# State-space layer: B times the step by TensorE for four states of three channel groups, and the norm one chunk later

## The chip, the cores and the metric

The kernel runs on one core of one Trainium2 chip. The metric is the time of the whole program on the device, in microseconds (us), as the median of several runs.

## What is computed

The program is a tower of nine layers over 8 images of 257 tokens with 256 channels. The change lies in one of them, a bidirectional state-space layer: the same recurrence runs over the tokens forward and backward, with weights of its own for each direction. Cut to what matters:

```python
xz = einsum('bld,ed->ble', x, Win);  u, z = split(xz, 2)      # 512 channels each
uc = silu(conv4(u));  x_dbl = uc @ Wx.T                       # rank 16, B 32, C 32
dt = softplus(x_dbl[..., :16] @ Wdt.T + bdt)
def step(h, ins):                                             # h: 512 channels x 32 states
    dt_t, B_t, C_t, u_t = ins
    h = exp(dt_t[..., None] * A) * h + (dt_t * u_t)[..., None] * B_t[:, None, :]
    return h, einsum('bdn,bn->bd', h, C_t)
y = (scan(step) + uc * Dp) * silu(z);  out = y @ Wout.T       # then a layer norm and Wfuse
```

## The kernel before

The state-space layer is `section_mamba`. It has 16 **units** `u`: 8 images forward, then 8 backward. In a unit the 512 channels are 4 groups `j` of 128 (one channel to a partition), and the 32 states are taken two at a time, so that a unit has 64 **pairs** `p`, 16 for each group. Four pairs are a **chunk** `n`; a unit has 16 chunks, numbered 0 to 15, and the inner counter `m` is 0 to 3. The work of a pair goes through all engines:

- ScalarE, `decay`: two exponentials give the decay `da` of the pair, one chunk ahead of VectorE.
- TensorE, `spread_b`: two bf16 matmuls put the two rows of B on all partitions, into one of the four PSUM buffers `pb`. It waits until the scan of pair p-4 has freed the buffer, and stands two pairs ahead of VectorE in the program.
- VectorE, `product`: multiplies that buffer by `dtu` (the step times u). It stands one pair ahead of the scan, so that VectorE's order is product p+1, scan p.
- VectorE, `tensor_tensor_scan`: runs the recurrence along 256 tokens for both states, and frees the buffer (`b_free`).
- GpSimd: multiplies the result by C, two pairs at a time (`hc`).
- TensorE, `total`: adds the products of each state into `py`, two chunks behind.

Each engine has its own instruction list, executed in order, and the order is written out by hand in its `body`: at fixed places (n, m) the list of unit u also holds the preparation of unit u+1 (projections `project`, `b_c_rank`, `time_step`, convolution, softplus) and the rest of unit u-1 (`outward`, the norm's `variance`, `fuse`, and on ScalarE `take_out`, `square`, `root`, `affine`). Three places matter below:

- ScalarE opens chunk 7 with `take_out(u-1)`, which waits for TensorE's `outward` of chunk 6 (m = 3).
- ScalarE's `decay` calls in chunk 15 belong to chunk 0 of unit u+1, and the first waits for the step of the next unit (`dt_set`), which GpSimd makes in `soften` behind its own chunk 13.
- Units 1 to 6 and 9 to 14 stand in two loops of three rounds of two units.

The parts of ScalarE's list that the places stand in, as before:

```python
if n == 7 and before is not None:
    take_out(u - 1)
...
for m in range(4):
    ...
    if n + 1 < NCH:
        decay(u, v, d, n + 1, m, free)
    elif after is not None:
        decay(u + 1, 1 - v, after, 0, m, free)
```

Of the kernel before, what the change touches and what calls it, by code (L numbers as in the profile page):

```python
# [23 lines left out]
P = 128  # L24
B = 8
# [1195 lines left out]
def section_mamba(nc, k, con, dirs, bfuse, normed=0):  # L1221
# [5 lines left out]
    UN = 2 * B  # L1227
    L = T - 1
    open_section(nc, k, "mamba")
    with ExitStack() as ctx:  # L1230
# [22 lines left out]
        y_l = sb("yl", [P, 2, DJ])  # L1253
        e1, e2 = sb("e1", [P, DJ, T]), sb("e2", [P, DJ, T])
# [3 lines left out]
        names = ("w_first w_in w_ready eye_set rates in_back out_back x_in proj_done proj_free lead uc_done xd_done xd_out part_set part_cut stacked last_bc last_out rate_l decay_l sum_l y_last z_last dt_done "  # L1258
# [7 lines left out]
        def image(u, d):  # L1266
            return u - B * d

# [29 lines left out]
        with nc.Block() as block:  # L1298
            @block.sync
            def _(sp):  # L1300
# [8 lines left out]
                sp.wait_ge(s["xd_done"], B)  # L1309
                sp.wait_ge(s["dt_done"], DJ * B)  # L1310
# [144 lines left out]
            def _(pe):  # L1455
# [37 lines left out]
                def spread_b(u, v, p):  # L1493

                    pe.wait_ge(s["b_free"], Turn(u, SUB, 4)(p - 3))
                    for o in range(2):
                        st = 2 * (p % (NS_ // 2)) + o
                        ins = nc.tensor.matmul(pb[:, p % 4, o, :], one_state(st), bst2[:, v, 0:L], start=True, stop=True)  # L1498
                    ins.then_inc(s["b_done"], 1)

                def total(u, v, d, n, m):
# [38 lines left out]
                def body(u, v, d, before, after):  # L1540
# [4 lines left out]
                    for n in range(NCH):  # L1545
                        for m in range(4):
# [6 lines left out]
                            elif before is not None:  # L1553
                                total(u - 1, 1 - v, before, NCH - 2 + n, m)
                            if n < QN:
                                spread_c(u, v, NQ_ * n + 2 * m)
                                spread_c(u, v, NQ_ * n + 2 * m + 1)
                            if after is not None:
# [19 lines left out]
                                if (n, m) == (14, 2):  # L1578
# [3 lines left out]
                            if before is not None:  # L1582
# [11 lines left out]
                                if (n, m) == (12, 2):  # L1594
                                    fuse(u - 1, 1)
                                if (n, m) == (13, 0):
# [10 lines left out]
                b_c_rank(0, 0)  # L1607
                for j in range(DJ):
# [19 lines left out]
            def _(act):  # L1628
# [4 lines left out]
                act.sem_inc(s["c_free"], 2)  # L1633

# [16 lines left out]
                def take_rank(u):  # L1651
# [3 lines left out]
                    nc.scalar.copy(part[:, 0, :], rank[0:2 * NS_, :]).then_inc(s["part_set"], 1)  # L1655

# [69 lines left out]
                def body(u, v, d, before, after):  # L1726
                    for n in range(NCH):
# [6 lines left out]
                        if n == 11 and before is not None:  # L1734
                            root(u - 1)
                        if n == 12 and before is not None:
                            affine(u - 1, before)
                        for m in range(4):
# [5 lines left out]
                            if n < QN:  # L1744
                                for o in range(2):
                                    st = NQ_ * n + 2 * m + o
                                    act.wait_ge(s["c_done"], Turn(u, NS_)(st + 1))
                                    nc.scalar.copy(cb[:, st, :], pm[:, st % 2, 0:L]).then_inc(s["c_free"], 1)  # L1748
                        if n == 1 and before is not None:
                            decay_last(u - 1)  # L1750
                        if after is not None:
# [7 lines left out]
                            if n == 9:  # L1759
                                take_rank(u + 1)  # L1760
                            if n == 10:
# [20 lines left out]
                take_rank(0)  # L1782
                act.wait_ge(s["w_in"], 16 * 12)
# [20 lines left out]
            def _(dve):  # L1804
# [47 lines left out]
                def product(u, v, p):  # L1852

                    j = p // (4 * QN)
# [6 lines left out]
                def body(u, v, d, before, after):  # L1861
                    for n in range(NCH):
                        q = n % QN
                        j = n // QN
                        for m in range(4):
# [8 lines left out]
                            dve.wait_ge(s["b_set"], Turn(u, SUB)(p + 1))  # L1874
# [4 lines left out]
                            if before is not None:  # L1879
# [4 lines left out]
                                if (n, m) == (11, 2):  # L1884
                                    scale(u - 1)
                                if (n, m) == (13, 2):
# [959 lines left out]
```

## Time and profile before

| | |
|---|---|
| median of 3 runs | 4415.77 us (4385.23 to 4431.04) |
| the profiled execution | 4409.2 us, its span 4407.5 us |
| the state-space layer in it | about 1547 to 3349 us, 1802 us |
| busy in that stretch | VectorE 1793.5, GpSimd 1627.7, TensorE 1580.0, ScalarE 1361.2 us |

The page sums over nine layers; only the stretch of the state-space layer is touched, and it is read by itself. Records of TensorE overlap each other (a matmul's end is modelled), so its pace is read from one start to the next, and so is VectorE's.

### The profile page before, as it was taken

The numbers are of one execution on the slowest core, as the hardware profiler recorded it, in microseconds if no ns is written. First come the engines' busy times: TensorE is split into PE (matmuls) and PEld (weight loads), VectorE is DVE, ScalarE is ACT, GpSimd is POOL, SyncE is SP. The second block draws the span as 40 slices with busy tenths as digits, with TensorE's granted clock in tenths as the row PEclk, the third lists the DMA queues.
The fourth block names the chain that finished last, engine by engine and source line by source line (L and its number), as shares of the span: only waits on it lengthen the run. The fifth ranks groups of instructions, "written<-read, shape, count | busy, mean of one in ns | idle before, by whom it ended". The sixth has DMA issues, their size and how long they took to land. (4 is left out here: it accounts for less than half of the span.)

```text
span 4407.5 us, 60885 instructions
## 1 busy us (share of the span) xinstructions
PE 3597.4 (82%) x19446; PEld 2461.4 (56%) x19446; DVE 2653.6 (60%) x3903; ACT 2062.6 (47%) x4702; POOL 1824.5 (41%) x1794
## 2 busy tenths in 40 slices
PE   2848848988798688888888889888887788888857
PEld 1625527555665456666666666666655655555534
DVE  6322233444322399999999999999996333333331
ACT  1211111222311377777777777777773233343322
POOL 0030020000100289999899999999983000000011
PEclk9669967999999899999999999999999999999965
DMA  3137730000247300000000000000000000000045
GB/s 88 49 135 273 271 105 1 1 1 1 104 149 267 113 1 1 1 2 1 2 13 1 1 3 1 2 1 2 1 1 10 24 1 1 1 1 1 1 142 170
DMA packets 94869, 214.40 MB, mean 49 GB/s; under 512 B 13792, under 2 KB 69088, under 8 KB 84224
## 3 DMA queue, kind: packets, MB, share of 16 engines
q1 hardware_dynamic: 71136, 177.89, 12.0%
q0 software_dynamic: 6400, 16.85, 1.2%
q10 hardware_dynamic: 16992, 15.47, 1.0%
q8 instruction: 170, 2.79, 0.3%
q14 instruction: 171, 1.40, 0.1%
HBM read 166.61 MB, written 43.56 MB: 48 GB/s over the span
## 5 line engine op out<-in xcount | busy, mean ns | idle before, releaser
L1876 DVE TENSOR_TENSOR_SCAN ssm_hs<-ssm_da,ssm_pb 128x512 f32<-128x512 f32 x1024 | 1240.0, 1211 | 3.6 <-ACT ssm_da L1715 3.6
L1415 POOL TENSOR_TENSOR ssm_hc<-ssm_hs,ssm_cb 128x1024 f32<-128x1024 f32 x512 | 1206.8, 2357 | 0.5 <-issue 0.5
L1512 PE MATMUL ssm_py<-ssm_hc,ident 128*128 128x256 f32 x4096 | 1062.1, 382 | 4.2 <-POOL ssm_hc L1415 4.1
L1715 ACT ACTIVATE ssm_da<-ssm_dt,ssm_an 128x255 f32<-128x255 f32 x2048 | 871.6, 503 | 133.3 <-POOL ssm_dtu L1363 89.8
L1512 PEld LDWEIGHTS ssm_py<-ssm_hc,ident 128*128 128x128 f32 x4096 | 706.4, 191 | 81.4 <-POOL ssm_hc L1415 7.1
L1859 DVE TENSOR_TENSOR ssm_pb<-ssm_pb,ssm_dtu 128x512 f32<-128x512 f32 x1024 | 693.5, 677 | 26.0 <-PE ssm_pb L1498 24.1
L1498 PE MATMUL ssm_pb<-ssm_bst,ssm_eyeb 96*128 96x256 bf16 x2048 | 404.0, 279 | 207.6 <-DVE ssm_hs L1876 192.1
L1498 PEld LDWEIGHTS ssm_pb<-ssm_bst,ssm_eyeb 96*128 96x128 bf16 x2048 | 148.2, 98 | 482.7 <-DVE ssm_hs L1876 407.1
L1114 DVE TENSOR_REDUCE duo_mxr<-duo_ring 128x4 f32<-128x1024 f32 x128 | 156.6, 1225 | 318.5 <-PE duo_ring L847 307.4
L2317 PE MATMUL moe_pu<-moe_up,moe_xt 128*128 128x512 f32 x568 | 273.0, 604 | 54.1 <-issue 52.5
L2214 POOL DMA_INDIRECT moe_yg<-moe_y_dram,moe_slot x51 | 48.7, 955 | 571.7 <-DMA moe_y_dram<-moe_yo 545.7
L2607 DVE COPY moe_ht<-moe_pz 128x512 f32<-128x512 f32 x71 | 49.1, 692 | 296.4 <-PE moe_pz L2327 296.4
L1748 ACT COPY ssm_cb<-ln_ps 128x256 f32<-128x256 f32 x512 | 166.0, 380 | 71.4 <-PE ln_ps L1484 70.5
L841 PE MATMUL duo_ring<-duo_k,duo_q 32*128 32x256 f32 x1024 | 148.0, 407 | 45.3 <-DVE duo_mxr L1114 45.0
L747 POOL TENSOR_TENSOR duo_qb<-duo_bm,duo_q 128x4 f32<-128x4 f32 x32 | 6.3, 196 | 427.3 <-ACT duo_k L989 427.3
L2317 PEld LDWEIGHTS moe_pu<-moe_up,moe_xt 128*128 128x128 f32 x568 | 98.6, 191 | 145.1 <-issue 142.3
L1005 ACT ACTIVATE duo_ex<-duo_ring 128x1024 f32<-128x1024 f32 x128 | 130.8, 1023 | 104.4 <-PE duo_ring L847 104.4
L747 POOL TENSOR_TENSOR lat_qb<-lat_bm,lat_q 128x4 f32<-128x4 f32 x32 | 6.4, 199 | 416.5 <-DVE lat_k L1102 416.5
L1414 POOL COPY ssm_hl<-ssm_hs 128x4 f32<-128x4 f32 x512 | 96.3, 188 | 149.5 <-DVE ssm_hs L1876 59.8
L841 PEld LDWEIGHTS duo_ring<-duo_k,duo_q 32*128 32x128 f32 x1024 | 94.8, 191 | 102.4 <-issue 48.0
L847 PE MATMUL duo_ring<-duo_q,duo_k 32*128 32x256 f32 x1024 | 147.7, 408 | 0.0
L1463 PE MATMUL ln_ps<-xb,ssm_win 128*128 128x257 f32 x512 | 133.7, 385 | 4.7 <-POOL xb L1324 2.6
(547 smaller groups left out, 5960.2 us busy)
## 6 DMA issues: line engine op xcount, KB each, us to landing
moe_up<-in_moe_up SPq DMA_DIRECT2D x72, 1024.0 KB, 5.2
moe_down<-in_moe_down SPq DMA_DIRECT2D x72, 512.0 KB, 6.0
moe_xr<-moe_x_dram SPq DMA_DIRECT2D x71, 128.0 KB, 5.8
moe_y_dram<-moe_yo ACTq DMA_DIRECT2D x71, 128.0 KB, 1.7
sw_wt<-in_sw_w SPq DMA_DIRECT2D x47, 192.5 KB, 2.5
sw_x_dram<-sw_zero SPq DMA_DIRECT2D x1, 6016.0 KB, 20.0
sw_xr<-sw_x_dram SPq DMA_DIRECT2D x47, 128.0 KB, 2.4
sw_y_dram<-sw_yo ACTq DMA_DIRECT2D x47, 128.0 KB, 1.7
```

The costliest lines, as they stand in the source:

```text
L841: ins1 = nc.tensor.matmul(dst1[:, o, at:at + w], q[r, b1, t * P:t * P + P], kk[r, b1, a, 0:w], start=not causal, stop=not causal or t == 1)
L847: ins2 = nc.tensor.matmul(dst2[:, o, at:at + 256 - q0], kk[r, b2, a, t * P:t * P + P], q[r, b2, q0:256], start=not causal, stop=not causal ...
L1114: ins = nc.vector.tensor_reduce(mxr[:, a, js, :], src.rearrange("p o (t s) -> p o t s", t=2), AX, ALU.max)
L1415: nc.gpsimd.tensor_tensor(hc[:, n % 2, part_], hs[:, n % 2, part_], cb[:, q * NQ_ + 4 * half:q * NQ_ + 4 * half + 4, :], ALU.mult).then_in ...
L1463: ins = nc.tensor.matmul(pm[:, n % 2, 0:T], w_in[:, c, n * P:n * P + P], k.xb[:, c, 0:T], start=(c == 0), stop=(c == C - 1))
L1498: ins = nc.tensor.matmul(pb[:, p % 4, o, :], one_state(st), bst2[:, v, 0:L], start=True, stop=True)
L1512: ins = nc.tensor.matmul(py[:, j % 2, 0:L], k.ident[:], hc[:, n % 2, st, :], start=False, stop=(q == QN - 1 and st == NQ_ - 1))
L1715: ins = nc.scalar.activation(da[:, n % 2, 2 * m + o, 1:L], dt2[:, v, j, 1:L], ACT.Exp, scale=a_n[:, d, j, st:st + 1])
L1748: nc.scalar.copy(cb[:, st, :], pm[:, st % 2, 0:L]).then_inc(s["c_free"], 1)
L1859: nc.vector.tensor_tensor(b2, b2, dtu2[:, v, j:j + 1, 0:L].broadcast_to([P, 2, L]), ALU.mult).then_inc(s["b_set"], 1)
L1876: nc.vector.tensor_tensor_scan(two(hs[:, n % 2, 2 * m:2 * m + 2, :]), two(da[:, n % 2, 2 * m:2 * m + 2, :]), two(pb[:, p % 4]), 0.0, ALU.m ...
L2317: ins = nc.tensor.matmul(pu[:, b % 2, g, :], xt[:, b % 2, c, :], up[:, b % WR, c, g * HID:g * HID + HID], start=(c == 0), stop=(c == C - 1))
```

## The change

In each unit the pairs 30, 31, 46, 47, 62 and 63 (the last four states of groups 1, 2 and 3) no longer pass through `product`. TensorE makes their input of the scan alone: `dtu` of the group, turned by two transposes (`turn_dtu`, into the free half of `py`) and copied to SBUF by ScalarE (`take_turned`), is multiplied by diagonal matrices that hold B of a state. ScalarE builds the diagonals (`build_diag`, eight activations a unit) from columns of B that TensorE computes once more (`b_columns`, eight matmuls) and ScalarE copies (`take_columns`). `root`, `affine`, `scale`, `add` and the two `fuse` of the unit before stand one chunk later (`variance` stays), and `spread_last` and `take_last` move from chunk 14 to chunk 15.

```diff
+        def on_tensor(p):
+            return p >= 4 * QN and p % (4 * QN) >= 4 * QN - NT // 2      # NT = 4, QN = 4
...
+                def b_columns(u, v):
+                    for h in range(2):
+                        for j in range(DJ):
+                            ins = nc.tensor.matmul(pm[:, 1, h * NT:h * NT + NT], uc2[:, v, j, h * P:h * P + P], w_x[:, j, NS_ - NT:NS_], start=(j == 0), stop=(j == DJ - 1))
+                    ins.then_inc(s["bt_done"], 1)
+                def turn_dtu(u, v, j):
+                    pe.wait_ge(s["ys_done"], Turn(u, DJ, 2)(j))
+                    pe.wait_ge(s["dt_set"], Turn(u, DJ)(j + 1))
+                    for h in range(2):
+                        ins = nc.tensor.transpose(py[:, (j + 1) % 2, h * P:h * P + P], dtu2[:, v, j, h * P:h * P + P], k.ident[:])
+                    ins.then_inc(s["tr_done"], 1)
...
                 def spread_b(u, v, p):
                     pe.wait_ge(s["b_free"], Turn(u, SUB, 4)(p - 3))
+                    if on_tensor(p):
+                        j, st = p // (NS_ // 2), 2 * (p % (NS_ // 2)) - (NS_ - NT)
+                        if st == 0:
+                            pe.wait_ge(s["tr_out"], Turn(u, DJ - 1, 1)(j))
+                            pe.wait_ge(s["diag_set"], u + 1)
+                        for h in range(2):
+                            ins = nc.tensor.matmul(pb[:, p % 4, :, h * P:h * P + P], dtu_t[:, j % 2, h, :], diag[:, v, h, st:st + 2, :], start=True, stop=True)
+                        ins.then_inc(s["b_done"], 1)
+                        return
...
+                            if n > QN and n % QN == 2 and m == 2:
+                                turn_dtu(u, v, n // QN)
...
                                 if (n, m) == (9, 0):
                                     b_c_rank(u + 1, 1 - v)
+                                    b_columns(u + 1, 1 - v)
...
-                                if (n, m) == (14, 2):
+                                if (n, m) == (15, 1):
                                     if before is not None:
                                         pe.wait_ge(s["f_out"], u + 2)
                                     spread_last(u + 1, 1 - v)
...
+                def build_diag(u, v, h):
+                    for st in range(NT):
+                        ins = nc.scalar.activation(diag[:, v, h, st, :], k.ident[:], ACT.Copy, scale=b_t[:, h, st:st + 1])
+                def take_turned(u, v, j):
+                    ...
+                    act.wait_ge(s["tr_done"], Turn(u, DJ - 1)(j))
+                    nc.scalar.copy(dtu_t[:, j % 2], py[:, (j + 1) % 2, 0:L].rearrange("p (h t) -> p h t", h=2)).then_inc(s["tr_out"], 1)
...
-                        if n == 11 and before is not None:
+                        if n == 12 and before is not None:
                             root(u - 1)
-                        if n == 12 and before is not None:
+                        if n == 13 and before is not None:
                             affine(u - 1, before)
...
+                            if n > QN and n % QN == QN - 1 and m == 1:
+                                take_turned(u, v, n // QN)
...
                                 soft_top(u + 1, 0, 4)
+                            if n == 15:
                                 take_last(u + 1, 1 - v)
+                            if n in (14, 15):
+                                build_diag(u + 1, 1 - v, n - 14)
...
                 def product(u, v, p):
+                    if on_tensor(p):
+                        return
```

Where the copies stand is told by the order of the built programs. ScalarE, a middle unit, from the copy of `take_out` at the head of chunk 7 on; `ssm_da` are the exponentials of `decay`, `ssm_zs` the gate of unit u+1. Before:

```order
L1690 COPY ln_cen<-ln_ps 128x514
L1710 REGISTER_ALU
L1712 REGISTER_ALU
L1715 ACTIVATE ssm_da<-ssm_dt,ssm_an 128x255 x2
L1712 REGISTER_ALU
L1715 ACTIVATE ssm_da<-ssm_dt,ssm_an 128x255 x2
L1712 REGISTER_ALU
L1715 ACTIVATE ssm_da<-ssm_dt,ssm_an 128x255 x2
L1712 REGISTER_ALU
L1715 ACTIVATE ssm_da<-ssm_dt,ssm_an 128x255 x2
```

And after the change:

```order
L1756 COPY ln_cen<-ln_ps 128x514
L1776 REGISTER_ALU
L1778 REGISTER_ALU
L1781 ACTIVATE ssm_da<-ssm_dt,ssm_an 128x255 x2
L1778 REGISTER_ALU
L1781 ACTIVATE ssm_da<-ssm_dt,ssm_an 128x255 x2
L1720 ISA
L1721 COPY ssm_dtut<-ssm_py 128x256
L1778 REGISTER_ALU
L1781 ACTIVATE ssm_da<-ssm_dt,ssm_an 128x255 x2
L1778 REGISTER_ALU
L1781 ACTIVATE ssm_da<-ssm_dt,ssm_an 128x255 x2
```

The copy of the turned step (`ssm_dtut`) stands behind the copy of `take_out` and four exponentials.

ScalarE, the same unit, chunk 15. Before, from `soft_top` and `take_last` (`ssm_bcl`) of chunk 14 on:

```order
L1686 ACTIVATE ssm_e<-ssm_e 128x1028
L1720 COPY ssm_bcl<-ln_ps 128x64
L1712 REGISTER_ALU
L1715 ACTIVATE ssm_da<-ssm_dt,ssm_an 128x255 x2
L1712 REGISTER_ALU
L1715 ACTIVATE ssm_da<-ssm_dt,ssm_an 128x255 x2
```

And after the change:

```order
L1752 ACTIVATE ssm_e<-ssm_e 128x1028
L1712 ACTIVATE ssm_diag<-ident,ssm_bt 128x128 x4
L1778 REGISTER_ALU
L1781 ACTIVATE ssm_da<-ssm_dt,ssm_an 128x255 x2
L1778 REGISTER_ALU
L1781 ACTIVATE ssm_da<-ssm_dt,ssm_an 128x255 x2
L1720 REGISTER_ALU
L1721 COPY ssm_dtut<-ssm_py 128x256
```

Here too the copy has come behind four exponentials, and these belong to the next unit.

TensorE, the same unit, chunks 6 and 7: `ssm_zs,ssm_wout` is `outward`, `ssm_dtu` the transposes, `ssm_diag` the new form of `spread_b`. After the change:

```order
L1498 MATMUL ssm_py<-ident,ssm_dtu 128x128 x2
L1564 MATMUL ln_ps<-ssm_zs,ssm_wout 128x257 x2
L1525 REGISTER_ALU
L1537 MATMUL ssm_pb<-ssm_bst,ssm_eyeb 128x256 x2
L1553 MATMUL ssm_py<-ssm_hc,ident 128x256 x2
L1564 MATMUL ln_ps<-ssm_zs,ssm_wout 128x257 x2
L1525 REGISTER_ALU
L1529 REGISTER_ALU
L1532 MATMUL ssm_pb<-ssm_diag,ssm_dtut 128x2x128 x2
L1553 MATMUL ssm_py<-ssm_hc,ident 128x256 x2
```

The second `outward` in these rows is the one that ScalarE's `take_out` waits for, and the next thing but registers on TensorE needs the copy that ScalarE makes after it.

## Rows read from the trace of the kernel before

**Rows 1.** One window: length, busy PE, PEld, DVE, ACT, POOL, granted clock, DMA

```profile
1547.00:3349.00 1802.00, 1579.99 (x7934) 1131.00 (x7933) 1793.49 (x2169) 1361.20 (x3339) 1627.68 (x1449) 0.99 0.01 2
```

**Rows 2.** Groups of instructions in that stretch (busy us, mean ns, idle before)

```profile
L1876 DVE TENSOR_TENSOR_SCAN ssm_hs<-ssm_da,ssm_pb 128x512 f32<-128x512 f32 x1024 | 1240.0, 1211 | 3.6 <-ACT ssm_da L1715 3.6
L1859 DVE TENSOR_TENSOR ssm_pb<-ssm_pb,ssm_dtu 128x512 f32<-128x512 f32 x1022 | 692.2, 677 | 4.1 <-PE ssm_pb L1498 2.2 <-issue 1.8
```

**Rows 3.** VectorE in order of time: product of pair 32, scan of pair 31, unit 4

```profile
2049.11 0.68 DVE L1859 TENSOR_TENSOR ssm_pb<-ssm_pb,ssm_dtu 128x512 f32<-128x512 f32 x1
2049.69 1.22 DVE L1876 TENSOR_TENSOR_SCAN ssm_hs<-ssm_da,ssm_pb 128x512 f32<-128x512 f32 x1
```

**Rows 4.** TensorE in order of time, chunks 6 to 8 of unit 4

```profile
2042.65 1.03 PE L1523 MATMUL ln_ps<-ssm_zs,ssm_wout 128*128 128x257 f32 x4
2043.52 0.38 PE L1498 MATMUL ssm_pb<-ssm_bst,ssm_eyeb 96*128 96x256 bf16 x2
2043.74 1.03 PE L1512 MATMUL ssm_py<-ssm_hc,ident 128*128 128x256 f32 x4
...
2052.64 1.03 PE L1463 MATMUL ln_ps<-xb,ssm_win 128*128 128x257 f32 x4
```

**Rows 5.** ScalarE in order of time, chunks 7 and 8 of unit 4

```profile
2043.72 0.59 ACT L1690 COPY ln_cen<-ln_ps 128x514 f32<-128x514 f32 x1 [4.89 <-PE ln_ps L1523]
2044.20 3.30 ACT L1715 ACTIVATE ssm_da<-ssm_dt,ssm_an 128x255 f32<-128x255 f32 x8
...
2056.35 3.30 ACT L1715 ACTIVATE ssm_da<-ssm_dt,ssm_an 128x255 f32<-128x255 f32 x8
```

**Rows 6.** TensorE elsewhere: four-column f32 matmuls, and transposes

```profile
3879.79 1.06 PE L860 MATMUL duo_ring<-duo_kb,duo_q 128*128 128x4 f32 x8
L2327 PE MATMUL moe_pz<-ident,moe_hid 128*128 128x128 f32 x284 | 42.6, 273 | 0.0
```

**Rows 7.** TensorE in order of time, chunk 9 of unit 4

```profile
2057.45 1.90 PE L1470 MATMUL ln_ps<-ssm_uc,ssm_wx 128*80 128x257 f32 x8
2059.19 0.38 PE L1498 MATMUL ssm_pb<-ssm_bst,ssm_eyeb 96*128 96x256 bf16 x2
```

**Rows 8.** ScalarE at the end of chunk 10, VectorE's scan of pair 47, unit 4

```profile
2069.32 0.41 ACT L1659 CAST ssm_part<-ssm_rank 64x257 bf16<-64x257 f32 x1 [0.63 <-POOL ssm_rank L1344]
2077.96 1.22 DVE L1876 TENSOR_TENSOR_SCAN ssm_hs<-ssm_da,ssm_pb 128x512 f32<-128x512 f32 x1
```

**Rows 9.** GpSimd and ScalarE in order of time, end of unit 4; who waited for L1363

```profile
2084.32 0.19 POOL L1414 COPY ssm_hl<-ssm_hs 128x4 f32<-128x4 f32 x1 [2.48 <-DVE ssm_hs L1876]
...
2101.80 1.27 POOL L1363 TENSOR_TENSOR ssm_dtu<-ssm_dt,ssm_uc 128x514 f32<-128x514 f32 x1
2103.19 4.09 ACT L1715 ACTIVATE ssm_da<-ssm_dt,ssm_an 128x255 f32<-128x255 f32 x10 [5.85 <-POOL ssm_dtu L1363]
  ACT ssm_da L1715: 89.8, 15
```

**Rows 10.** TensorE and VectorE in order of time, pairs 62 and 63 of unit 4

```profile
2099.14 0.39 PE L1498 MATMUL ssm_pb<-ssm_bst,ssm_eyeb 96*128 96x256 bf16 x2 [0.45 <-DVE ssm_hs L1876]
2104.70 1.22 DVE L1876 TENSOR_TENSOR_SCAN ssm_hs<-ssm_da,ssm_pb 128x512 f32<-128x512 f32 x1
2106.40 1.22 DVE L1876 TENSOR_TENSOR_SCAN ssm_hs<-ssm_da,ssm_pb 128x512 f32<-128x512 f32 x1
```

**Rows 11.** TensorE after idle gaps (heads of units 3 and 5), and windows as in Rows 1

```profile
1882.36 0.40 PE L1498 MATMUL ssm_pb<-ssm_bst,ssm_eyeb 96*128 96x256 bf16 x2 [3.00 <-DVE ssm_hs L1876]
1886.00:1888.00 2.00, 2.00 (x14) 1.59 (x13) 2.00 (x4) 1.42 (x5) 0.67 (x1) 0.99 0.00 0
...
2108.40 0.61 PE L1498 MATMUL ssm_pb<-ssm_bst,ssm_eyeb 96*128 96x256 bf16 x2 [2.88 <-DVE ssm_hs L1876]
2108.80 1.91 PE L1512 MATMUL ssm_py<-ssm_hc,ident 128*128 128x256 f32 x4
2112.00:2114.00 2.00, 2.00 (x8) 1.35 (x8) 1.43 (x2) 0.89 (x4) 0.83 (x1) 0.50 0.00 0
```

More of the change, by code:

```diff
@@ L1227, in section_mamba @@
     UN = 2 * B
+    NT = 4
     L = T - 1
@@ L1257, in section_mamba @@
         pm = k.ln_ps
-        names = ("w_first w_in w_ready eye_set rates in_back out_back x_in proj_done proj_free lead uc_done xd_done xd_out part_set part_cut stacked last_bc last_out rate_l decay_l sum_l y_last z_last dt_done "
+        names = ("bt_done bt_out tr_done tr_out diag_set w_first w_in w_ready eye_set rates in_back out_back x_in proj_done proj_free lead uc_done xd_done xd_out part_set part_cut stacked last_bc last_out rate_l decay_l sum_l y_last z_last dt_done "
                  "dt_free dt_exp dt_set c_done c_free b_done b_free da_done b_set hc_done y_free ys_done o_done o_out "
@@ L1267, in image, with on_vector @@
             return u - B * d
+        def on_tensor(p):
+            return p >= 4 * QN and p % (4 * QN) >= 4 * QN - NT // 2
+        def on_vector(p):
+            return sum(1 for x in range(p + 1) if not on_tensor(x))
+        NV = on_vector(SUB - 1)
         def one_state(n):
@@ L1475, in time_step @@
                         pe.wait_ge(s["xd_out"], u + 1)
+                    if j == 1:
+                        pe.wait_ge(s["bt_out"], u + 1)
                     r = slice(2 * NS_, 2 * NS_ + RK)
@@ L1607, in _ @@
                 b_c_rank(0, 0)
+                b_columns(0, 0)
                 for j in range(DJ):
@@ L1655, in take_rank, with take_columns @@
                     nc.scalar.copy(part[:, 0, :], rank[0:2 * NS_, :]).then_inc(s["part_set"], 1)
+                def take_columns(u):
+                    act.wait_ge(s["bt_done"], u + 1)
+                    nc.scalar.copy(b_t[:].rearrange("p h n -> p (h n)"), pm[:, 1, 0:2 * NT]).then_inc(s["bt_out"], 1)
+                def build_diag(u, v, h):
+                    if h == 0:
+                        act.wait_ge(s["bt_out"], u + 1)
+                    for st in range(NT):
+                        ins = nc.scalar.activation(diag[:, v, h, st, :], k.ident[:], ACT.Copy, scale=b_t[:, h, st:st + 1])
+                    if h == 1:
+                        ins.then_inc(s["diag_set"], 1)
+                def take_turned(u, v, j):
+                    used = Turn(u, SUB)(4 * QN * (j - 1))
+                    if not isinstance(u, int) or used > 0:
+                        act.wait_ge(s["b_done"], used)
+                    act.wait_ge(s["tr_done"], Turn(u, DJ - 1)(j))
+                    nc.scalar.copy(dtu_t[:, j % 2], py[:, (j + 1) % 2, 0:L].rearrange("p (h t) -> p h t", h=2)).then_inc(s["tr_out"], 1)
                 def second(u):
@@ L1794, in _ @@
                     decay(0, 0, 0, 0, m, None)
+                for h in range(2):
+                    build_diag(0, 0, h)
                 units(act, body)
@@ L1873, in body @@
                             dve.wait_ge(s["da_done"], Turn(u, SUB)(p + 1))
-                            dve.wait_ge(s["b_set"], Turn(u, SUB)(p + 1))
+                            if on_tensor(p):
+                                dve.wait_ge(s["b_done"], Turn(u, SUB)(p + 1))
+                            else:
+                                dve.wait_ge(s["b_set"], Turn(u, NV)(on_vector(p)))
                             two = lambda ap: ap.rearrange("p s t -> p (s t)")
```

17 lines of the change are left out of this document (13 added, 4 removed).

## The prediction

> **What bounds the kernel now.** I read the windows first: in the 1802 us of the state-space layer VectorE is busy 1793.5 us, GpSimd 1627.7, TensorE 1580.0 and ScalarE 1361.2 [rows 1]. Then the groups: of VectorE's 1024 scans one waited noticeably, 3.6 us in all, and the products waited 4.1 us in all [rows 2]. So VectorE sets the end, and any time taken from it shows, as long as nothing else comes late. Its records overlap, so its pace is read from start to start: a product takes 0.58 us (2049.11 to 2049.69) and two scans with one product between them lie 1.70 us apart (2104.70 to 2106.40), which leaves 1.12 us for a scan [rows 3, 10]. TensorE's idle time is slack in small pieces, not free time at any place: it is to deliver the input of a pair at most two pairs ahead, and the sum hangs on where it must wait. Therefore I walked unit 4 instruction by instruction on the timelines of all four engines.
>
> **What is taken away.** Six products a unit, 96 in all, at 0.58 us: 56 us of VectorE. If nothing else moved, that would be the gain.
>
> **What TensorE gets.** Four passes of an f32 matmul over 256 or 257 columns take 0.87 us (2042.65 to 2043.52), the bf16 pair that they replace 0.22 us (2043.52 to 2043.74) [rows 4]. An f32 matmul is two passes, so each of the six spreads costs 0.65 us more. The eight matmuls of `b_columns` are 16 passes with four columns; eight such passes take 1.06 us to the last one's end, so I take 1.9 us. The transposes are two passes for each group; a pass of this form costs 0.15 us (42.6 us over 284), together 0.3 us [rows 6]. That is about 6.7 us a unit. It fits into a unit of 112.6 us (1802 over 16), and the question is only where.
>
> **What ScalarE gets.** Three copies of 128x256 from PSUM (a 128x514 one hands over after 0.48 us, 2043.72 to 2044.20 [rows 5]; I take 0.4 us), eight small activations that build the diagonals, and one tiny copy. The diagonals stand in chunks 14 and 15, on either side of the wait of 5.85 us for GpSimd [rows 9], and I cost them at nothing; without that cover they would be some 3 us a unit at the 0.4 us of an exponential (3.30 us for 8 [rows 5]). The norm's move takes no work away or adds any.
>
> **What the waits cost: the copy of the turned step.** The first spread of each pair of spreads (30, 46, 62) waits for ScalarE's copy, and all of TensorE's list stands behind it, the `spread_b` of pairs 32 and 33 among it. VectorE's product of pair 32 stands ahead of the scan of 31, so it waits for those too.
>
> Group 1 (A). ScalarE begins chunk 7 with `take_out`, which already waits 4.89 us for TensorE's `outward` [rows 5]. It would start at 2043.72 plus 0.3 for the transposes, hand over after 0.48, run four exponentials at 0.4 and the copy: 2044.0 + 0.5 + 1.6 + 0.4 + 0.1 = 2046.6. TensorE wanted to go on at 2043.52 [rows 4]. From 2046.6 on it has spread, `total`, spread, `total`, `project` (five times 0.86) and the bf16 pair (0.22) before product 32 can start: 2051.1. Product and start of scan 31: 2051.8. The scan started at 2049.69 [rows 3]. A = +2.1 us, with the two saved products already counted.
>
> Knock-on (B). The projections of unit u+1 stand behind. The last started at 2052.64 [rows 4] and now has, from 2051.1, pairs 32 to 35 in its way: about 2057.0. ScalarE's exponentials for chunk 9 started at 2056.35, 3.7 us after it [rows 5], now at 2060.7, and the first pair is there at 2061.5. VectorE wants it for pair 36 five pairs after 2051.8, at 2060.4. B = +1.1 us.
>
> `b_columns` (C). It stands behind the 1.74 us of `b_c_rank` (2057.45 to 2059.19 [rows 7]). By then TensorE has no lead left: from 2061.1 it has 1.74 + 1.9 us before the spread of pair 39, ready at 2064.95, where VectorE would want it at 2064.3. C = +0.7 us. Where A doesn't occur, TensorE's lead hides it.
>
> Group 2 (D). ScalarE's chunk 10 ends at 2069.7 [rows 8]; four exponentials and the copy give 2071.85. Spread, `total`, `time_step` (0.63), spread, `total`, `variance` and the pair are 5.15 us, so product 48 starts at 2077.0 and scan 47 at 2077.6 against 2077.96 [rows 8], and that one had `scale` (0.58) before it, which now comes later. D = 0: the stall eats the saving.
>
> Group 3 (E). Here the copy stands behind ScalarE's wait for GpSimd, 89.8 us in 15 waits [rows 9]. GpSimd works without a wait from 2084.32 to the end of L1363, so an earlier norm doesn't bring it forward. ScalarE starts at 2103.19, and four exponentials, the copy and 0.1 give 2105.3. TensorE wanted pair 62 at 2099.14 [rows 10]. From 2105.3: spread, `total`, spread, `total`, pair (3.66), product and hand-over (0.7): scan 63 starts at 2109.6 against 2106.40 [rows 10], +3.2 us. But TensorE has then been idle for over 6 us. After gaps of 2.88 and 3.00 us its granted clock was 0.50, the level of 1.2 GHz instead of 2.4: a pair took 0.40 instead of 0.22 us; it was back at 0.99 some 4 us after the one gap and still at 0.50 more than 3.6 us after the other [rows 11]. At half speed in the first 3.4 to 5.6 us the chain is 1.7 to 2.8 us longer; I take 2.4. E = +5.6 us.
>
> The Trainium skill (TensorE: Matmul & The Clock Gate, The HAM clock gate) says that the low clock is the array's default and activity releases it. The trace agrees, with the 0.50 above. By the opposite view, a clock that stays, the unit's sum would be 7.1 instead of 9.5.
>
> **The sum.** A + B + C + D + E = 9.5 us for each of the 14 middle units: 133 us. Unit 0 has no `take_out` (group 1 and 2 gain 1.2 each) but has E: about +3.5. The last unit has no next one: no E, about -1. Together +135 us. The profiled execution (4409.2 us) lies 0.15% under the median, so I add 135 to 4415.8: **4550 us**, 3.1% slower.
>
> **Rivals.**
> - *The clock stays up in group 3.* 7.1 x 14 is 99, and the rest cancels: 4515 us. For it: TensorE was densely busy before the gap. Against: both shown gaps were less than half as long.
> - *The clock falls in group 1 as well.* The gap there would be 2043.9 to 2046.6, 2.6 us, just under the 2.88 that did it. Then 1.7 to 3.1 us more in 14 units: about 4585 us.
> - *Only group 3 stalls.* If VectorE's buffers and ScalarE absorb groups 1 and 2, a unit gives -2.3 + 5.6 = +3.3: 4465 us; with the clock up -2.3 + 3.2: about 4430 us, within 1%. For it: TensorE has on average a third of each pair's time free. Against: four passes beside each pair of chunk 6 and 7 use just that.
> - *On the other side: TensorE's lead covers the copies.* Then the 96 products are all gain: 4360 us. It decides in group 3: scan 63 is not late if the spread of 62 begins by 2101.0, which takes the step of GpSimd 4.3 us earlier than 2103.07. For it: `root` no longer holds ScalarE in chunk 11, so the softplus could come sooner. Against: GpSimd had no idle time there that could be saved.
>
> **How the numbers follow.** Chances: forecast 0.48, clock up 0.14, clock down twice 0.18, only group 3 with the clock down 0.05 and up 0.03, something unforeseen that cancels it 0.05, the copies covered 0.07. The range leaves out the last two and reaches past the dearest: 4460 to 4610. About 1% (44 us) is what a measurement of this kernel can tell from no change. Faster by more: 0.07 (the covered case). Within: 0.08. Slower: 0.85.
>
> **What would show it.** In the changed profile TensorE's new spreads (`ssm_diag`) should be listed with idle time before them on ScalarE's copy (`ssm_dtut`): near 2.5 us in chunk 7, 2 us in chunk 11, 6 us and more in chunk 15. VectorE's scans and products in that stretch should wait about 150 to 200 us for TensorE, against 4 before, and the granted clock of the layer should fall from 0.99 to about 0.94. The layer should last about 1935 us, and everything outside it what it did. The prediction is wrong if the spread of pair 62 isn't held by the copy, or if VectorE's order leaves it work that I took for waiting.

## The result, and the profile after

| | before | after |
|---|---|---|
| median | 4408.05 us (4 runs, 4385.23 to 4431.04) | 4542.46 us (4 runs, 4524.54 to 4576.56) |
| ratio (that of the two medians is 1.0305) | | 1.0314, 95% interval 1.0228 to 1.0400: slower |
| the profiled execution | 4409.2 us | 4531.75 us |
| first to last scan of the layer in it | 1800.4 us | 1949.3 us |

The predicted time was 4550 us, in a range of 4460 to 4610. The layer itself, from its first scan to its last, grew by 149 us; between the two profiled executions only 123 us are left of it. The first scan of the layer lies at 1547.15 us in one and at 1527.53 in the other, with nothing changed ahead of it, and in the nine profiled executions of this study it lies anywhere from 1519 to 1560: that is scatter from one execution to the next. So the layer is compared below, scan by scan.

The layer's window, which answers to [rows 1] (same columns):

```profile
1527.00:3478.00 1951.00, 1669.59 (x8453) 1258.80 (x8452) 1748.10 (x2073) 1416.89 (x3531) 1628.45 (x1448) 0.97 0.01 2
```

VectorE is busy 45 us less and the stretch is 149 us longer: it now has some 203 us without work. Its groups in that window, which answer to [rows 2], and the new spreads:

```profile
L1958 DVE TENSOR_TENSOR_SCAN ssm_hs<-ssm_da,ssm_pb 128x512 f32<-128x512 f32 x1024 | 1232.4, 1209 | 85.7 <-PE ssm_pb L1532 68.2 <-ACT ssm_da L1781 15.3 <-issue 2.2
...
L1938 DVE TENSOR_TENSOR ssm_pb<-ssm_pb,ssm_dtu 128x512 f32<-128x512 f32 x926 | 628.2, 678 | 120.2 <-PE ssm_pb L1537 118.5
...
L1532 PE MATMUL ssm_pb<-ssm_diag,ssm_dtut 128*128 128x256 f32 x384 | 125.6, 457 | 168.1 <-ACT ssm_dtut L1721 132.7 <-issue 20.9 <-DVE ssm_hs L1958 14.5
```

The 96 products less are there (1022 to 926 in the two windows, 692.2 to 628.2 us). The waits of the layer from 1540 us on (engine, buffer and line that waited, for whom: us in all, times, longest) name the chain: VectorE waits for TensorE, TensorE for ScalarE's copy L1721, and ScalarE, in front of some of those copies, for `outward` (L1564) or for GpSimd:

```profile
PE ssm_pb L1532 <- ACT ssm_dtut L1721: 132.7, 36, 6.9
...
DVE ssm_pb L1938 <- PE ssm_pb L1537: 116.2, 64, 3.1
...
ACT ssm_da L1781 <- POOL ssm_dtu L1376: 88.6, 15, 6.7
ACT ln_cen L1756 <- PE ln_ps L1564: 77.7, 15, 6.1
DVE ssm_hs L1958 <- PE ssm_pb L1532: 68.2, 30, 4.6
```

Now unit 4 in order of time, as the prediction walked it. **Group 1**, chunk 7, ScalarE, against [rows 5]:

```profile
2063.28 0.59 ACT L1756 COPY ln_cen<-ln_ps 128x514 f32<-128x514 f32 x1 [5.10 <-PE ln_ps L1564]
2063.76 1.70 ACT L1781 ACTIVATE ssm_da<-ssm_dt,ssm_an 128x255 f32<-128x255 f32 x4
2065.37 0.35 ACT L1721 COPY ssm_dtut<-ssm_py 128x256 f32<-128x256 f32 x1
...
2079.99 2.50 ACT L1781 ACTIVATE ssm_da<-ssm_dt,ssm_an 128x255 f32<-128x255 f32 x6
```

TensorE at the same place, against [rows 4], then its new `b_columns`, and the same place in unit 9:

```profile
2062.21 1.03 PE L1564 MATMUL ln_ps<-ssm_zs,ssm_wout 128*128 128x257 f32 x4
2065.77 1.13 PE L1532 MATMUL ssm_pb<-ssm_diag,ssm_dtut 128*128 128x256 f32 x4 [2.53 <-ACT ssm_dtut L1721]
...
2070.20 0.38 PE L1537 MATMUL ssm_pb<-ssm_bst,ssm_eyeb 96*128 96x256 bf16 x2
...
2082.14 1.84 PE L1490 MATMUL ln_ps<-ssm_wx,ssm_uc 128*128 128x4 f32 x16
2083.84 0.38 PE L1537 MATMUL ssm_pb<-ssm_bst,ssm_eyeb 96*128 96x256 bf16 x2
...
2679.72 2.08 PE L1532 MATMUL ssm_pb<-ssm_diag,ssm_dtut 128*128 128x256 f32 x4 [2.53 <-ACT ssm_dtut L1721]
2681.59 1.73 PE L1553 MATMUL ssm_py<-ssm_hc,ident 128*128 128x256 f32 x4
```

VectorE there, against [rows 3]: product 32, scan 31, and the scan of pair 36 in the knock-on:

```profile
2070.62 0.70 DVE L1938 TENSOR_TENSOR ssm_pb<-ssm_pb,ssm_dtu 128x512 f32<-128x512 f32 x1 [2.39 <-PE ssm_pb L1537]
2071.23 1.21 DVE L1958 TENSOR_TENSOR_SCAN ssm_hs<-ssm_da,ssm_pb 128x512 f32<-128x512 f32 x1
...
2081.08 1.22 DVE L1958 TENSOR_TENSOR_SCAN ssm_hs<-ssm_da,ssm_pb 128x512 f32<-128x512 f32 x1 [0.98 <-ACT ssm_da L1781]
```

The copy starts at 2065.37, behind `take_out` and four exponentials, and the spread begins 2.49 us after the start of `take_out` (2.6 in the prediction). VectorE's product waits 2.39 us for a bf16 spread that did nothing but stand behind the stalled one. **Group 2**, end of chunk 10 and chunk 11: ScalarE, TensorE, and VectorE's product 48 and scan 47, against [rows 8]:

```profile
2093.03 0.41 ACT L1725 CAST ssm_part<-ssm_rank 64x257 bf16<-64x257 f32 x1 [0.64 <-POOL ssm_rank L1357]
...
2094.95 0.35 ACT L1721 COPY ssm_dtut<-ssm_py 128x256 f32<-128x256 f32 x1
```

```profile
2095.35 1.13 PE L1532 MATMUL ssm_pb<-ssm_diag,ssm_dtut 128*128 128x256 f32 x4 [1.64 <-ACT ssm_dtut L1721]
```

```profile
2101.03 0.70 DVE L1938 TENSOR_TENSOR ssm_pb<-ssm_pb,ssm_dtu 128x512 f32<-128x512 f32 x1 [2.15 <-PE ssm_pb L1537]
2101.63 1.21 DVE L1958 TENSOR_TENSOR_SCAN ssm_hs<-ssm_da,ssm_pb 128x512 f32<-128x512 f32 x1
```

**Group 3**, chunk 15: ScalarE, then TensorE, then VectorE's scans 62 and 63 with product 64 of the next unit between, against [rows 9, 10]:

```profile
2127.05 1.70 ACT L1781 ACTIVATE ssm_da<-ssm_dt,ssm_an 128x255 f32<-128x255 f32 x4 [5.87 <-POOL ssm_dtu L1376]
2128.66 0.35 ACT L1721 COPY ssm_dtut<-ssm_py 128x256 f32<-128x256 f32 x1
```

```profile
2129.06 2.07 PE L1532 MATMUL ssm_pb<-ssm_diag,ssm_dtut 128*128 128x256 f32 x4 [6.89 <-ACT ssm_dtut L1721]
2130.93 1.91 PE L1553 MATMUL ssm_py<-ssm_hc,ident 128*128 128x256 f32 x4
2132.63 1.44 PE L1532 MATMUL ssm_pb<-ssm_diag,ssm_dtut 128*128 128x256 f32 x4
2133.91 1.03 PE L1553 MATMUL ssm_py<-ssm_hc,ident 128*128 128x256 f32 x4
```

```profile
2131.24 1.22 DVE L1958 TENSOR_TENSOR_SCAN ssm_hs<-ssm_da,ssm_pb 128x512 f32<-128x512 f32 x1 [3.36 <-PE ssm_pb L1532]
2135.24 0.70 DVE L1938 TENSOR_TENSOR ssm_pb<-ssm_pb,ssm_dtu 128x512 f32<-128x512 f32 x1 [2.78 <-PE ssm_pb L1537]
2135.85 1.21 DVE L1958 TENSOR_TENSOR_SCAN ssm_hs<-ssm_da,ssm_pb 128x512 f32<-128x512 f32 x1
```

A pass here is one of TensorE's records: an f32 matmul has two of them. After 6.89 us without work TensorE's four passes take 1.87 us from start to start (2129.06 to 2130.93) instead of 0.87: the lower of its two clock levels, as two windows over it show (columns as in [rows 1]; the granted clock is the third number from the end):

```profile
2129.00:2131.00 2.00, 1.94 (x5) 1.58 (x6) 0.00 (x0) 1.61 (x5) 2.00 (x3) 0.50 0.00 0
2134.00:2136.00 2.00, 2.00 (x14) 1.59 (x13) 0.76 (x2) 0.99 (x4) 0.00 (x0) 1.00 0.04 8
```

The next four still take 1.70; full speed comes back within the spread at 2132.63, which takes 1.28.

**Unit 0**, ahead of its scan 16: ScalarE's diagonals, TensorE's next entry for C behind them and VectorE's product behind that, and the same TensorE entry in the kernel before:

```profile
1529.73 2.43 ACT L1712 ACTIVATE ssm_diag<-ident,ssm_bt 128x128 f32<-128x128 f32 x8
...
1533.26 0.66 PE L1514 MATMUL ln_ps<-ssm_cst,ssm_eyeb 96*128 96x256 bf16 x2 [4.93 <-ACT ssm_cb L1814]
...
1534.39 0.70 DVE L1938 TENSOR_TENSOR ssm_pb<-ssm_pb,ssm_dtu 128x512 f32<-128x512 f32 x1 [2.22 <-PE ssm_pb L1537]
...
1550.55 0.66 PE L1484 MATMUL ln_ps<-ssm_cst,ssm_eyeb 96*128 96x256 bf16 x2 [2.60 <-ACT ssm_cb L1748]
```

Here all eight diagonals stand in one piece ahead of ScalarE's copies of C (`ssm_cb`), for which TensorE waits 2.33 us longer than before. (This is read from the two traces; no run moved the diagonals.)

### The profile page after: what moved, and what is told of

It reads as the page before. It is cut to its first block and busy times, and to the rows that moved or that the text cites. A ratio compares the mean times of both kernels' runs of the same rounds, so it can differ in the third digit from the quotient of the medians.

```text
span 4529.9 us, 62642 instructions
## 1 busy us (share of the span) xinstructions
PE 3657.8 (81%) x19990; PEld 2571.9 (57%) x19990; DVE 2608.6 (58%) x3807; ACT 2118.6 (47%) x4894; POOL 1827.2 (40%) x1794
## 5 line engine op out<-in xcount | busy, mean ns | idle before, releaser
L1781 ACT ACTIVATE ssm_da<-ssm_dt,ssm_an 128x255 f32<-128x255 f32 x2048 | 878.2, 504 | 135.2 <-POOL ssm_dtu L1376 88.6
L1553 PEld LDWEIGHTS ssm_py<-ssm_hc,ident 128*128 128x128 f32 x4096 | 719.2, 192 | 81.5 <-POOL ssm_hc L1428 0.4
L1938 DVE TENSOR_TENSOR ssm_pb<-ssm_pb,ssm_dtu 128x512 f32<-128x512 f32 x928 | 629.5, 678 | 145.4 <-PE ssm_pb L1537 143.6
L1537 PE MATMUL ssm_pb<-ssm_bst,ssm_eyeb 96*128 96x256 bf16 x1856 | 362.5, 277 | 110.8 <-DVE ssm_hs L1958 101.3
L1532 PE MATMUL ssm_pb<-ssm_diag,ssm_dtut 128*128 128x256 f32 x384 | 125.6, 457 | 168.1 <-ACT ssm_dtut L1721 132.7
L1532 PEld LDWEIGHTS ssm_pb<-ssm_diag,ssm_dtut 128*128 128x128 f32 x384 | 80.8, 226 | 204.1 <-ACT ssm_dtut L1721 147.2
L1005 ACT ACTIVATE duo_ex<-duo_ring 128x1024 f32<-128x1024 f32 x128 | 130.9, 1024 | 104.4 <-PE duo_ring L847 104.4
```

What stands on the lines that cost most here:

```text
L1005: released(nc.scalar.activation(ex[:, (ua * 2 + 1 - jp) % NE], bank("s2", u, a, jp)[:, :, 0:SW], ACT.Exp, scale=scale), "s2", u, a, jp)
L1532: ins = nc.tensor.matmul(pb[:, p % 4, :, h * P:h * P + P], dtu_t[:, j % 2, h, :], diag[:, v, h, st:st + 2, :], start=True, stop=True)
L1553: ins = nc.tensor.matmul(py[:, j % 2, 0:L], k.ident[:], hc[:, n % 2, st, :], start=False, stop=(q == QN - 1 and st == NQ_ - 1))
L1781: ins = nc.scalar.activation(da[:, n % 2, 2 * m + o, 1:L], dt2[:, v, j, 1:L], ACT.Exp, scale=a_n[:, d, j, st:st + 1])
L1938: nc.vector.tensor_tensor(b2, b2, dtu2[:, v, j:j + 1, 0:L].broadcast_to([P, 2, L]), ALU.mult).then_inc(s["b_set"], 1)
```

## The experiments

One measure serves them all. From VectorE's timeline the starts of the 1024 scans are read, and a middle unit is cut at some of them. A middle unit, without the extra at loop heads and without the units in which the clock fell in group 1 (with the products gone, in group 3), in us (no profile shows this table; it is worked out from the starts). After the change scans 56 to 63 have two values, for the units alternate between them:

| kernel | scans 24 to 31 | 31 to 36 | 36 to 40 | 40 to 56 | 56 to 63 | first to last scan of the layer |
|---|---|---|---|---|---|---|
| before | 12.29 | 8.54 | 6.84 | 29.05 | 12.29 | 1800.4 |
| after | 14.48 | 9.86 | 7.20 | 29.33 | 17.7 or 18.2 | 1949.3 |
| copies early | 11.68 | 9.85 | 7.20 | 27.73 | 11.88 | 1789.2 |
| copy early, group 3 only | 14.48 | 9.86 | 7.20 | 29.33 | 11.88 | 1860.8 |
| array kept busy | 14.48 | 9.86 | 7.20 | 29.33 | 16.1 | 1927.3 |
| products gone | 11.09 | 8.94 | 6.84 | 27.86 | 11.09 | 1756.7 |
| norm only | 12.29 | 8.54 | 6.83 | 28.26 | 13.08 | 1800.0 |
| groups 2 and 3 | 12.29 | 8.54 | 6.84 | 27.74 | 11.88 | 1775.5 |
| the same, columns later | 12.29 | 8.54 | 6.83 | 27.73 | 11.88 | 1773.9 |

The step `add` (0.8 us, 13.08 less 12.29) stands in "40 to 56" before and in products gone, and in "56 to 63" in all others. The ratios of the first four experiments are to 29 runs of the kernel before (median 4398.74 us), those of the last three to 23 (4393.96).

**1. All three copies early.** Is it the place of the copy in ScalarE's list, or TensorE's additional work?

```diff
+                        if n > QN and n % QN == QN - 1 and n // QN in (1, 2, 3):
+                            take_turned(u, v, n // QN)
                         if n == 7 and before is not None:
                             take_out(u - 1)
...
-                            if n > QN and n % QN == QN - 1 and m == 1:
-                                take_turned(u, v, n // QN)
```

> The changed kernel, but in groups 1, 2 and 3 ScalarE copies the turned step at the very head of chunks 7, 11 and 15, ahead of take_out and of the exponentials; nothing else differs. Theory (the place of the copy is the cost): TensorE's new spreads wait under 20 us in all for the copy (about 140 in the changed kernel), a middle unit takes 109.5 to 111.5 us from first scan to first scan (121.8 changed, 112.2 before), the layer about 1770 us (1949 changed, 1800 before), the ratio to the kernel before 0.985 to 0.995. Rival (TensorE's added 6.7 us of work a unit is the cost, wherever it waits): a unit stays over 115 us and the ratio over 1.01.

Measured: 4391.67 us, ratio 0.9981 (0.9945 to 1.0017). The layer took 1789.2 us, 160 less than after the change, with every added operation still in it. The place of the copy was the cost; but the layer is 19 us longer than expected and the ratio above 0.995, so the added work isn't free either. Its unit 4 in order of time: ScalarE's exponentials of chunk 9 and its copy in group 3; TensorE's spread in group 1, and the one behind the copy in group 3; VectorE's product 32, and scan 36 at the knock-on:

```profile
2030.13 3.29 ACT L1781 ACTIVATE ssm_da<-ssm_dt,ssm_an 128x255 f32<-128x255 f32 x8
...
2069.65 0.35 ACT L1721 COPY ssm_dtut<-ssm_py 128x256 f32<-128x256 f32 x1
```

```profile
2016.03 1.02 PE L1532 MATMUL ssm_pb<-ssm_diag,ssm_dtut 128*128 128x256 f32 x4
...
2071.36 1.10 PE L1532 MATMUL ssm_pb<-ssm_diag,ssm_dtut 128*128 128x256 f32 x4 [0.63 <-DVE ssm_hs L1958]
```

```profile
2020.77 0.70 DVE L1938 TENSOR_TENSOR ssm_pb<-ssm_pb,ssm_dtu 128x512 f32<-128x512 f32 x1 [0.47 <-PE ssm_pb L1537]
...
2031.23 1.22 DVE L1958 TENSOR_TENSOR_SCAN ssm_hs<-ssm_da,ssm_pb 128x512 f32<-128x512 f32 x1 [0.97 <-POOL ssm_hc L1428]
```

In group 3 the copy is done before the buffer is free, and the spread waits for VectorE, as in the kernel before. ScalarE still waits 84.8 us for GpSimd in the layer; nothing of that reaches VectorE any more.

What is left lies in three places. In group 1 the spread doesn't wait at all, TensorE works without a gap, and even so product 32 waits 0.47 us for it: scans 24 to 31 take 11.68 us, where two products less would make 11.1. In group 2 product 48 waits 0.56 us for TensorE in unit 4, and scans 40 to 47 take 11.75 us, where norm only (12.29) less two products would be 11.1. The third is chunk 9: scan 36 waits 0.97 us here, too. The row names a GpSimd product as the last releaser, but ScalarE's start lies 1.10 us ahead of the scan here and 1.09 after the change, so it is the exponential; its start stands 8.75 us behind scan 31 here, 8.76 after the change and 6.66 before. So the knock-on doesn't come from the copy's wait; it is TensorE's longer list in front of the projections, two f32 spreads and the transposes. From scan 24 to scan 36 this kernel takes 1.5 us more than the one without the products (21.53 against 20.03), and that is what the list has more: two spreads at 0.65 and two passes of transposes, 0.22 us in all.

**2. The six products gone, and nothing in their place**, to see what the idea can be worth at most. It is the kernel before, with the same six pairs left out of `product` (so the input of their recurrence lacks the factor `dtu`, and the result is not the layer's) and the scan waiting for the spread there:

```diff
+        def on_tensor(p):
+            return p >= 4 * QN and p % (4 * QN) >= 4 * QN - 2
...
                 def product(u, v, p):
+                    if on_tensor(p):
+                        return
...
-                            dve.wait_ge(s["b_set"], Turn(u, SUB)(p + 1))
+                            if on_tensor(p):
+                                dve.wait_ge(s["b_done"], Turn(u, SUB)(p + 1))
+                            else:
+                                dve.wait_ge(s["b_set"], Turn(u, NV)(on_vector(p)))
```

> The kernel before with the six products of a unit left out and nothing in their place, so that the input of the recurrence lacks the factor dtu for four states of three groups. It shows what 96 products are worth. Theory (VectorE bounds the layer, 0.58 us each): layer 56 us shorter, about 1745 us, ratio 0.987. Rival (something else is close behind VectorE: GpSimd or the multiplication by C): under 30 us, ratio over 0.993.

Measured: 4347.46 us, ratio 0.9911 (0.9875 to 0.9947); the layer 1756.7 us. The ceiling is 44 us, not 56. Scans 31 to 36 take 8.94 instead of 8.54 us, for VectorE is now early enough to wait for the exponentials of chunk 9 (0.31 us in unit 4); that is some 5 of the 12 us. The rest goes in units 2 to 5 and 10 to 14, at the loop heads and right behind them, where the granted clock falls more often than before (nine times in the layer behind its start, against six); what makes it fall there was not tried.

**3. Only the norm moved**, in the kernel before:

```diff
-                        if n == 11 and before is not None:
+                        if n == 12 and before is not None:
                             root(u - 1)
...
-                                if (n, m) == (13, 2):
+                                if (n, m) == (14, 2):
                                     add(u - 1, before)
```

> The kernel before with only the second part of the change: root, affine, scale, add, both fuse and the last token's spread and copy one chunk later. Theory: no work is added, VectorE never waits for it: layer within 5 us of 1800, ratio 0.997 to 1.003. Rival: it takes a cover away or frees ScalarE in chunk 11: more than 10 us either way.

Measured: 4396.18 us, ratio 0.9993 (0.9963 to 1.0024), the layer 1800.0. By itself the later norm costs nothing and brings nothing.

**4. The array kept busy in group 3's gap**, by twelve f32 matmuls ahead of the wait, into the buffer that the spread then overwrites (24 passes). It parts the clock's share from the wait's own.

```diff
+                        if st == 0 and j == 3:
+                            for _ in range(12):
+                                nc.tensor.matmul(pb[:, p % 4, 0, :], k.ident[:], w_out[:, 0, 0, :], start=True, stop=True)
                         if st == 0:
                             pe.wait_ge(s["tr_out"], Turn(u, DJ - 1, 1)(j))
```

> The changed kernel, and in group 3 TensorE runs twelve f32 matmuls of 256 columns (5.1 us at full clock) into the free buffer before it waits for the copy; they end before the copy is there. Theory (the clock falls during the wait in group 3 and costs 1.7 to 2.8 us a unit there): from scan 56 to scan 63 a middle unit takes 15.5 to 16.5 us instead of 18.2, the layer 25 to 40 us less than the changed kernel's 1949. Rival (the clock is no cost in that place, the wait alone is): 18 us as before, and the layer within 5 us of 1949.

Measured: 4517.13 us, ratio 1.0272 (1.0209 to 1.0334), the layer 1927.3. TensorE and VectorE in group 3 of unit 4:

```profile
2119.62 5.45 PE L1530 MATMUL ssm_pb<-ssm_wout,ident 128*128 128x256 f32 x24 [0.45 <-DVE ssm_hs L1961]
2126.06 1.13 PE L1535 MATMUL ssm_pb<-ssm_diag,ssm_dtut 128*128 128x256 f32 x4 [1.00 <-ACT ssm_dtut L1724]
2127.03 1.03 PE L1556 MATMUL ssm_py<-ssm_hc,ident 128*128 128x256 f32 x4
```

```profile
2130.70 1.21 DVE L1961 TENSOR_TENSOR_SCAN ssm_hs<-ssm_da,ssm_pb 128x512 f32<-128x512 f32 x1
```

The spread waits for the same copy, and what follows runs at full speed: 4.64 us from the spread to scan 63, against 6.79 after the change. So 2.1 us of group 3's cost were the clock's (2.4 in the prediction), and the other part stays. 24 discarded passes made the layer 22 us shorter; 25 to 40 were expected. Scans 56 to 63 take 1.8 us less on average in the 14 middle units, 26 us; some of it was lost again in group 1, where the clock fell in five units instead of three.

**5. The copy early in group 3 alone.** What does each place cost?

```diff
+                        if n > QN and n % QN == QN - 1 and n // QN in (3,):
+                            take_turned(u, v, n // QN)
...
-                            if n > QN and n % QN == QN - 1 and m == 1:
+                            if n > QN and n % QN == QN - 1 and m == 1 and n // QN in (1, 2):
```

> The changed kernel with one copy moved: in group 3 alone ScalarE copies the turned step at the head of chunk 15, ahead of the next unit's exponentials; groups 1 and 2 as in the changed kernel. Theory (half of the loss is group 3's copy behind GpSimd's step): the stretch from scan 56 to scan 63 takes 11.9 us instead of 18.2 in a middle unit, the stretches before it stay (14.5 or 16.1, 9.9, 7.2, 13.35 us), the layer is about 1855 us, the ratio to the kernel before about 1.012. Rival (TensorE is late at the unit's end from groups 1 and 2 anyway): the stretch stays above 15 us and the layer above 1900.

Measured: 4472.54 us, ratio 1.0186 (1.0140 to 1.0231), the layer 1860.8. It is 88 us less than after the change and 72 more than with all copies early: group 3 is 55% of the damage, groups 1 and 2 with the clock's falls in them the rest. The layer came out as expected (1855), the ratio higher than 1.012: slower beyond doubt, but not told from 2%.

**6. The copies early, and group 1 back on VectorE**, since the knock-on stands behind group 1. Against the first experiment, without the semaphore counts that follow from it:

```diff
-            return p >= 4 * QN and p % (4 * QN) >= 4 * QN - NT // 2
+            return p >= 8 * QN and p % (4 * QN) >= 4 * QN - NT // 2
```

> As the run with all copies early, but only groups 2 and 3 have two pairs on TensorE; group 1 is as in the kernel before. Theory (around chunks 7 to 9 TensorE and ScalarE have no room, since outward, the projections and the gate stand there; in groups 2 and 3 they have): scans 31 to 36 take 8.54 us again instead of 9.85, scans 24 to 31 12.29, a middle unit outside the loop heads about 110.3 us against 112.2, the layer 1765 to 1775 us, the ratio 0.992 to 0.995. Rival (b_columns' work in chunk 9 is what costs, whichever groups use it): scans 36 to 40 stay at 7.2 and more, and the gain over the run with all groups is under 5 us.

Measured: 4381.08 us, ratio 0.9964 (0.9935 to 0.9993), the layer 1775.5. Scans 31 to 36 are back at 8.54 us, and 24 to 31 at 12.29, as expected; the layer is at the upper end of what was expected, the ratio above it. The gain over the first experiment is 13.7 us of layer, more than the rival's 5.

**7. The same with `b_columns` two pairs later**, at (9, 2), away from `b_c_rank`; against the sixth experiment:

```diff
                                 if (n, m) == (9, 0):
                                     b_c_rank(u + 1, 1 - v)
+                                if (n, m) == (9, 2):
                                     b_columns(u + 1, 1 - v)
```

> As the run with groups 2 and 3, with b_columns two pairs later (chunk 9, m = 2 instead of 0), no longer right behind b_c_rank. Theory (b_columns costs 0.36 us a unit because it stands behind 1.74 us of b_c_rank): scans 36 to 40 take 6.84 us, the layer up to 5 us less than the run with groups 2 and 3. Rival (VectorE has slack there once group 1 is gone, so nothing was lost): the same layer within 2 us.

Measured: 4372.84 us, ratio 0.9957 (0.9928 to 0.9986), the layer 1773.9. It is the best of the kernels that compute everything, and under the kernel before by less than one per cent. Against the sixth the layer differs by 1.6 us, which is no difference. This is the rival that was named, not the theory: `b_columns` cost 0.3 us in three units at its old place, and at the new one the stretch from 40 to 47 takes 0.25 more in the same number.

## Why the prediction was right

Each term for a middle unit, predicted and measured (from the table, `add` brought to the same side):

| term | predicted | measured |
|---|---|---|
| A, group 1, scans 24 to 31 | +2.1 | +2.2 |
| B, knock-on, 31 to 36 | +1.1 | +1.3 |
| C, `b_columns`, 36 to 40 | +0.7 | +0.4 |
| D, group 2, 40 to 56 | 0 | +1.05 |
| E, group 3, 56 to 63 | +5.6 | +4.6 or +5.2 |
| sum | 9.5 | 9.6 or 10.2 |

- **The mechanism** held: the copy's place behind other work of ScalarE's, in all three groups. The early copies take back 160 us, with the same instructions on every engine. How much of it is ScalarE's waits ahead of the copy and how much its four exponentials was not parted. The rival "the lead covers the copies" is out as the change stands; with the copies early it is true of the copies, but not of its gain of 56 us. The layer then is 11 us shorter than before and not the 44 of the ceiling, because an undisturbed unit takes 111.5 us with TensorE's work in it and 109.1 without (scan 0 to scan 0): 0.6 us in group 1, 0.9 in the knock-on, 0.4 at `b_columns` and 0.6 in group 2.
- **The total** is nearer than its terms, and that is in part luck. The layer grew by 149 us, not 135: group 2 (some 15 us) and the ends (7) cost more than forecast, group 3 less. The medians grew by 134, which is nearer to 135 than runs of one kernel are to each other.
- **A** held with its working, row by row. The clock fell after this gap in 3 of 14 units (1, 7 and 9), for 1.5 to 1.7 us each. That is the rival "the clock falls in group 1 as well", with 5 us instead of its 24 to 43.
- **B** had the right size for a reason that was half right. The prediction put it behind A's wait. The first experiment shows it without that wait: the list in front of the projections had become longer by itself. The second parts it: 0.4 us come with VectorE being earlier, the other 0.9 with TensorE's list.
- **C** was mis-sized: sixteen four-column passes take 1.70 us (2082.14 to 2083.84), not 1.9. The rest, 0.1 us, was not looked into: while B holds VectorE 0.2 us longer than predicted, TensorE may draw ahead. "Where A doesn't occur, TensorE's lead hides it" was wrong: with all copies early it is the same 0.4 us. It vanishes in 11 of the 14 units once group 1 is back on VectorE (sixth experiment).
- **D** is the step that failed: "the stall eats the saving" was right only for the wait. The norm's `scale` (0.58 us) had left this stretch, so to come out even scan 47 should have been 0.58 us earlier. The prediction's own working gave 0.36 earlier, hence +0.2, and the other 0.8 are the time from scan 40 to ScalarE's cast (0.5 more) and the chain from the cast (0.3 more: the spread came 2.3 us after the cast's start instead of 2.5, but product 48 started 5.68 us after the spread, not 5.15). The stretch ahead of the stall ran without lead, too: with early copies 0.6 us of the loss stay.
- **E** was nearly exact where it was walked, in unit 4: 2.01 us from ScalarE's start to the spread (2.1), and 6.79 from there to scan 63 (6.76). The total is lower since `add` came into this stretch and vanished in the wait; in unit 0, which has no `add`, E is 6.1.
- **The ends.** Unit 0 was longer by 8.6 us instead of 3.5. 2.3 of them lie ahead of scan 16 and are there with early copies too: they are the diagonals, which the prediction cost at nothing since they stand beside ScalarE's wait for GpSimd. In unit 0 eight of them (2.43 us) stand behind that wait and ahead of the copies of C, and TensorE waits 4.93 us there instead of 2.60. In the other units the cover held: ScalarE's waits for GpSimd are 88.6 us in 15, against 89.8. Behind scan 16, unit 0 has 0.6 us of B, 0.5 of C and in group 2 none of its gain of 1.2, though it has no `take_out`. The last unit gave +0.7 instead of -1. The 14 units between made 139.7 us, 10.0 each, the falls of the clock in group 1 (5 us) and less at the loop heads (some 3 us) among them; together they are the layer's 149.
- **What would show it.** VectorE's waits for TensorE: 184 us from 1540 us on (150 to 200 said). The spread's waits: 2.53, 1.64 and 6.89 us (2.5, 2, over 6). The layer: 1949 (1935). The granted clock was 0.97, not 0.94. The 0.94 did not follow from the working: 3.4 to 5.6 us at half speed in a unit of 122 take 0.01 to 0.02 off 0.99. In unit 4 the clock was already at 0.50 in the last 2 us of the gap (2127 to 2129), and then for 4.4 us of work.
- **The chances.** The range was said to leave out the last two cases, but it leaves out a third, "only group 3, clock up" at 4430 us with 0.03.

The Trainium skill (TensorE: Matmul & The Clock Gate, The HAM clock gate) has the low clock as the array's default, which activity releases. The rows of group 3 agree on both sides: 1.87 us for the four passes behind 6.89 us of idleness, and 0.97 (2126.06 to 2127.03) in the fourth experiment, where the gap was filled.

What stays open: why the clock fell in group 1 of some units and not of others, and why the chain behind group 2's spread took 5.68 us and not 5.15.

## What to carry to other kernels

A small instruction that another engine waits for costs what stands in front of it in its own engine's list. Look for the waits ahead of it there before adding up durations: here three copies of 0.35 us in a unit decided about 160 us, and moving one call a few lines up returned them. The same holds for work put beside a wait as a cover: look at the first and the last round, where the wait may stand elsewhere. If a moved operation sits in a stretch that already runs without slack, "the saving pays for the stall" is only true after everything else that was moved into or out of that stretch has been counted. And before building an exchange between engines, measure its ceiling with the work simply left out: 44 us here, of which the best version tried got 27.

## What the runs showed of the hardware that was not expected

- **The same gap can keep or lose TensorE's clock.** After 2.53 us without work the spread in group 1 took 0.97 us to the next start in unit 4 (2065.77 to 2066.74) and 1.87 in unit 9, with the same list of instructions ahead of it. Two windows over it (columns as in [rows 1]) show the granted clock:

```profile
2063.00:2069.00 6.00, 3.47 (x17) 2.87 (x16) 4.46 (x5) 5.33 (x11) 5.39 (x6) 1.00 0.00 1
2678.00:2684.00 6.00, 4.28 (x12) 3.54 (x13) 3.39 (x3) 4.55 (x10) 5.92 (x5) 0.72 0.00 0
```

  Judged by the length of scans 24 to 31 it fell in 3 of the 14 middle units after the change, in 5 with the copy early in group 3 and in 5 with the array kept busy in group 3.
- **A four-column f32 pass isn't nearly free.** 16 of them took 1.70 us, 0.11 us each, half of the 0.22 of a pass with 256 columns.
- **Runs of the kernel before differ by nearly 2%** (4358.43 to 4436.25 us in the 29 of them beside the first experiments), while stretches in which nothing waits repeat within 0.02 us from unit to unit and, where nothing is changed, from kernel to kernel (scans 24 to 31: 12.29 in all 14 middle units of four of the kernels). So a change of a few us a layer could be read from the scans when the medians couldn't tell it.
